# The second query group's output projection goes to the next attention unit, and the steps around it are numbered anew

## What is computed

```python
def reference(x, w_qkv, w_out, wg, w1, b1, w2, b2):
    xn = layernorm(x)
    ...
    qkv = einsum('bse,ehd->bshd', xn, w_qkv);  q, k, v = split(qkv, 3, axis=-1)
    logits = einsum('bqhd,bkhd->bhqk', q, k) / sqrt(64)
    probs = softmax(where(tril, logits, neg), axis=-1)
    attn = einsum('bshd,hde->bse', einsum('bhqk,bkhd->bqhd', probs, v), w_out)
    ...
    return x + attn + ffn
```

## Time and profile before

| | us |
|---|---|
| median of 3 runs | 3245.05 |
| lowest and highest | 3241.91, 3245.84 |
| the profiled execution | 3247.3 |
| span of its instructions | 3245.3 |
| PE busy | 3037.0 (94%) |
| DVE busy | 2254.5 (69%) |
| ACT busy | 1674.7 (52%) |
| POOL busy | 1612.6 (50%) |

### The profile page before, as it was taken

One profiled execution on the slowest core, in us unless ns is written; L12 is line 12 of the kernel. 1 busy time (PEld: TensorE's weight loads), 2 busy tenths in 40 slices (PEclk: granted clock), 3 DMA queues, 4 the chain that ended last, 5 costly groups with the idle time before them and its releaser, 6 DMA issues.

```text
span 3245.3 us, 64713 instructions
## 1 busy us (share of the span) xinstructions
PE 3037.0 (94%) x22677; PEld 2426.4 (75%) x22677; DVE 2254.5 (69%) x5152; ACT 1674.7 (52%) x3798; POOL 1612.6 (50%) x2384
## 2 busy tenths in 40 slices
PE   5589999999989999999999999999999999999996
PEld 3479998999977777777777777777777777777774
DVE  6844444444347778778877877787788778777875
ACT  2444444444445555555555555555555555555553
POOL 2132221222136665666566566656665665666563
PEclk7799999999999999999999999999999999999999
DMA  6022221222123323333233333333332333333232
GB/s 207 32 78 75 72 72 56 65 74 77 51 63 78 96 76 100 89 87 105 73 100 78 100 80 94 100 79 92 85 100 73 100 97 84 83 90 98 70 90 71
DMA packets 205201, 274.70 MB, mean 85 GB/s; under 512 B 61520, under 2 KB 161872, under 8 KB 204896
## 3 DMA queue, kind: packets, MB, share of 16 engines
q1 hardware_dynamic: 180288, 203.51, 22.6%
q0 software_dynamic: 24608, 67.17, 7.7%
HBM read 102.80 MB, written 33.55 MB: 42 GB/s over the span
## 4 chain that ended last, share of the span: by engine, by line
PE 55%; ACT 6%; DVE 5%; issue 4%; SPq 1%; DMA 0%; DVEq 0%
PE S L1272 14%; PE O L1309 13%; PE S L1188 8%; PE T L1285 8%; ACT pr L1347 4%; PE W L1223 3%; PE S L1203 3%; PE W L1203 3%; PE W L1188 3%; DVE pr L1404 2%; DVE kl L1435 1%; ACT kh L1362 1%; DVE ol L1449 1%; SPq L1125 1%; ACT oh L1372 1%
## 5 line engine op out<-in xcount | busy, mean ns | idle before, releaser
L1347 ACT ACTIVATE pr<-pr,negm 128x128 f32<-128x128 f32 (+7 forms) x1024 | 787.2, 770 | 756.5 <-DVE negm L1404 755.3
L1549 POOL TENSOR_SCALAR pr<-pr,rinv 128x128 f32<-128x128 f32 (+7 forms) x1024 | 759.6, 749 | 828.8 <-DVE rinv L1410 821.4
L1404 DVE CUSTOM_DVE_ANT_0 pr<-S,late 128x128 f32<-128x128 f32 (+7 forms) x1024 | 731.0, 751 | 48.1 <-PE S L1272 40.5
L1309 PE MATMUL O<-pT,vv 128*64 128x256 f32 (+1 forms) x5120 | 558.0, 364 | 14.0 <-DMA pT<-squares 13.2
L1309 PEld LDWEIGHTS O<-pT,vv 128*64 128x64 f32 x5120 | 345.7, 137 | 203.8 <-issue 24.1
L1339 DVE COPY pT<-T 128x512 f32<-128x512 f32 (+3 forms) x704 | 364.1, 540 | 147.3 <-PE O L1309 147.3
L1285 PE MATMUL T<-ident,pr 128*128 128x128 f32 x2688 | 420.6, 281 | 19.2 <-DVE pT L1339 18.6
L886 DVE TENSOR_TENSOR hl<-h,hh 128x512 fp32r<-128x512 f32 x256 | 191.5, 748 | 317.7 <-ACT hh L847 310.6
L1285 PEld LDWEIGHTS T<-ident,pr 128*128 128x128 f32 x2688 | 295.8, 140 | 133.5 <-issue 95.5
L843 ACT ACTIVATE h<-pH,b1c 128x512 f32<-128x512 f32 x256 | 175.9, 687 | 366.9 <-PE pH L773 353.0
L1272 PE MATMUL S<-kh,qh 64*128 64x512 f32 (+2 forms) x1536 | 319.6, 407 | 39.0 <-DVE negm L1404 34.9
(11 more groups left out here) (186 smaller groups left out, 6543.5 us busy)
## 6 DMA issues: line engine op xcount, KB each, us to landing
pT<-squares SPq DMA_DIRECT2D x768, 128.0 KB
pT<-squares POOLq DMA_DIRECT2D x256, 128.0 KB
y<-yb SPq DMA_DIRECT2D x128, 128.0 KB, 1.7
wr<-in_L_attn_w_qkv SPq DMA_DIRECT2D x128, 128.0 KB, 2.3
x<-in_L_attn_x SPq DMA_DIRECT2D x16, 512.0 KB, 5.4
xn<-xn SPq DMA_DIRECT2D x16, 512.0 KB, 5.1
w1r<-in_L_ffn_w SPq DMA_DIRECT2D x8, 1024.0 KB
w2r<-in_L_ffn_w SPq DMA_DIRECT2D x8, 1024.0 KB
```

The costliest lines, as they stand in the source:

```text
L1309: ins = e.matmul(O[hs, a:GQ], vv[n // 2 % 2][:, kt, vs], turned_p, start=(kt == 0), stop=(kt == KT - 1))
L1347: e.activation(pr[i][:, 0:w], pr[i][:, 0:w], ACT.Exp, bias=negm[:, i:i + 1], scale=-1.0, accum_out=rsum[:, i:i + 1]).then_inc(expd.sem, 1)
L1404: e.tensor_tensor_reduce(pr[i][:, 0:w], S[s % 2][:, off:off + w], late[:, SEQ - w:], 1.0, -MASKED, ALU.add, ALU.min, negm[:, i:i + 1]).the ...
L1549: e.tensor_scalar(pr[i][:, 0:width(s)], pr[i][:, 0:width(s)], rinv[:, i:i + 1], 1.0, ALU.mult, ALU.mult).then_inc(scaled.sem, 1)
```

## The change

The output projection o1 of group 1 leaves step 15 of its own unit and stands at step 2 of the next one (`NEXT = 1`: groups 1 to 3 are projected in the next unit, before it was 2 and 3). Its reader on DVE, the store of that quarter of the result and its refill follow. All the tables are new with it: o1's neighbours, `BANK_OF`, `AFTER` (group 0 at step 12 instead of 13, group 2 at step 6 of the next unit instead of 3), `SQUARE_LAG` 4 instead of 3, `POOL_AT`, and the chunks that ACT copies: eight instead of five, with 23 of a unit's 42 blocks instead of 10. No arithmetic is added or taken away.

```diff
-    KEPT_BY_ACT = {1, 10, 11, 13, 15}
+    KEPT_BY_ACT = {3, 7, 10, 11, 12, 13, 14, 15}
     KEPT_BY_DVE = set(range(CHUNKS)) - KEPT_BY_ACT
...
-    STEP_OF = {'p0': 0, 'v0': 1, 'xn': 1, 'v1': 4, 'p1': 6, 'p2': 6, 'p3': 6, 'o2': 9, 'o3': 12, 'o0': 14, 'o1': 15}
-    BANK_OF = {'p0': 0, 'p1': 1, 'p2': 0, 'p3': 2, 'o2': 2, 'xn': 0, 'v0': 2, 'o3': 2, 'v1': 0, 'o0': 2, 'o1': 2}
+    STEP_OF = {'p0': 0, 'v0': 0, 'o1': 2, 'p1': 3, 'p2': 3, 'p3': 4, 'v1': 4, 'xn': 7, 'o2': 8, 'o3': 12, 'o0': 14}
+    BANK_OF = {'p0': 0, 'p1': 0, 'p2': 1, 'p3': 2, 'o2': 2, 'xn': 2, 'v0': 2, 'o3': 2, 'v1': 1, 'o0': 2, 'o1': 2}
+
+    NEXT = 1
+    done_in = lambda n, g: n + (g >= NEXT)
...
-    POOL_AT = {'place0': 2, 'place1': 3, 'fetch0': 5, 'fetch1': 6, 'weigh': 9, 'add': 11, 'total': 15, 'split_w': 7, 'split_wv': 5}
+    POOL_AT = {'place0': 1, 'place1': 2, 'fetch0': 2, 'fetch1': 5, 'weigh': 8, 'add': 9, 'total': 13, 'split_w': 7, 'split_wv': 5}
...
-        SQUARE_LAG = 3
+        SQUARE_LAG = 4
...
-        AFTER = [13, 14, 19, 27]
+        AFTER = [12, 14, 22, 27]
...
                 if b > 0 and u == 0:
                     refill(b, 0)
-                    refill(b, 1)
...
                 if b > 0 and u == 0:
+                    store(b - 1, 1)
+                    refill(b, 1)
                     store(b - 1, 2)
...
                 if u == PAIRS - 1:
                     store(b, 0)
-                    store(b, 1)
...
-                of = n if g < 2 else n - 1
+                of = n if g < NEXT else n - 1
```

More of the change, by code:

```diff
@@ L947, in pieces @@
         there = {"p": n + 1 < UNITS, "x": n + AHEAD < TILES, "v": n + 1 < UNITS}
-        return [p for p in STEP_OF if there.get(p[0], n < UNITS if p in ("o0", "o1") else n > 0)]
+        return [p for p in STEP_OF if there.get(p[0], n < UNITS if p[0] == "o" and int(p[1]) < NEXT else n > 0)]
     class Pieces:
@@ L1127, in store @@
             def store(b, g):
-                e.wait_ge(dve.sem, dve.at(b * PAIRS + PAIRS - 1 + g // 2, f"o{g}"))
+                e.wait_ge(dve.sem, dve.at(done_in(b * PAIRS + PAIRS - 1, g), f"o{g}"))
                 e.dma_start(outv[:, b, 2 * g:2 * g + 2], res[:, 2 * g:2 * g + 2]).then_inc(stored[g].sem, 16)
@@ L1170, in _ @@
                     store(b, 0)
-                    store(b, 1)
             place(UNITS - 1)
-            for g in range(HT // 2, GROUPS):
+            for g in range(NEXT, GROUPS):
                 store(BATCH - 1, g)
@@ L1366, in group @@
                 e.wait_ge(pv.sem, pv.at(n, g + 1))
[L1368 to L1371, removed]
+                m, last = (n, g - 2) if g >= 2 else (n - 1, g + 2)
+                if m >= 0:
+                    e.wait_ge(filled.sem, filled.at(done_in(m, last), f"o{last}"))
                 e.activation(oh[g % 2][:], O[:], ACT.Copy).then_inc(ohi.sem, 1)
```

## The result

| | before | after |
|---|---|---|
| median, us | 3245.31 (3241.91 to 3245.84) | 3226.53 (3223.47 to 3228.04) |
| span of the profiled execution | 3245.3 | 3225.4 |
| ratio, 95% interval | | 0.9944 (0.9931 to 0.9956) |

The kernel is faster by 0.56%, 18.8 us of the forecast 44, with the right sign and less than half of the size. 3201 was the forecast and 3226.5 lies in the stated range, between the estimates for a late ACT (B, 3217) and a late DVE (C, 3233), but neither is what happened.

A forecast was written before the change was run, and what follows sets the result against it. PE was taken to bound the attention part, with its waits as the room. -0.66 - 0.20 + 0.20 = -0.66 us a unit, times 64 = -42.2, with the end -44, gave 3201 us from 3245.05; range 3172 to 3234.

The forecast's parts named there:

- B: Rival: ACT late at the unit's start, wait at chunk 12 0.45 us, net gain 0.41 a unit, 3217 us; chance 0.15.
- C: Rival: DVE late at step 8, 0.5 us more at step 10's scores, net gain 0.16 a unit, 3233 us; chance 0.08.
- PE bounds the attention part, and the waits decide, not DVE's load: Attention part: PE busy 34.3 of 35.7 us a unit; a new order can give back only its 1.4 us idle.
- rival E: DVE's copies, not the waits, decide: 13 blocks fewer, 2.2 us a unit, to about 3104 us; chance 0.02.
- The term of o1: Unit's end: PE's wait for group 1's remainder ol goes when o1 moves, -0.66 us a unit.
- The term of chunk 7: Step 9's transposes: with chunk 7's copy on ACT, row maxima start earlier and the wait for chunk 8 falls, -0.20 of 0.28 us.
- The wait at chunk 12: Transposes of step 10: PE newly waits for ACT's copy of chunk 10, +0.20 us a unit, bounds 0 and 0.5.
- The scores of step 10: PE's wait for step 9's row maximum stays at 0.43 us; term 0, bounds -0.1 and +0.5.
- Squares later: Squares one step later: placing DMAs still in time for group 3, distance about 12.7 us, some 2 us to spare; cost 0.
- Rival D: Placing DMAs become the bound at group 3: 3238 us, or slower at 3288; chances 0.03 no change or small gain, 0.09 slower.
- The changed neighbours: PE's starts where groups have new neighbours: may cost or give 0.1 us; cost 0.
- same work: Group 0's values stand ahead of chunk 7's transposes instead of behind them; counted at cost 0.

The follow-up runs named there:

- Experiment 2: The kernel before with only the new split of the chunk copies (ACT eight chunks, DVE eight): 3263.7 us, 1.0062.
- o1_early: `defer_xn` with o1 one step earlier, at step 1 behind xn instead of step 2: 3161.7 us, 0.9749 of the kernel before.
- Experiment 1: The kernel before with o1 alone moved to step 2 of the next unit, all other tables old: 3211.7 us, 0.9901.
- experiment 3: The changed kernel, two separate runs: squares back at three steps behind, 3219.1 us; or gathers back at steps 5 and 6, 3216.6 us.
- experiment 4: The changed kernel with the old split of the chunk copies (ACT 1, 10, 11, 13, 15) put back: 3283.0 us, 1.0125 of the changed kernel's predecessor.
- experiment 8: The changed kernel with squares at three steps, gathers late, and transposes of chunks 10 and 11 behind the next unit's first scores: 3175.7 us, 0.9794.
- g0_first: The kernel with o1 alone moved, plus group 0's values at step 12 instead of 13, ahead of chunk 7's transposes: 3238.3 us, 0.9986.
- experiment 5: The changed kernel with squares at three steps, old steps and banks of all pieces but o1, group 2's values at step 3: 3253.3 us, 1.0035.
- only_kept: The run of Experiment 2: the kernel before with only the new split of the chunk copies, 3263.7 us.
- fetch_late: The changed kernel with the gathers back at steps 5 and 6, their weighting at 9 and sum at 11: 3216.6 us, 0.9920.
- defer_xn: o1 alone moved, plus transposes of chunks 10 and 11 behind the next unit's first scores and xn in bank 1: 3170.0 us, 0.9772.

## Why the prediction was right and wrong, step by step

**PE bounds the attention part, and the waits decide, not DVE's load: right.** Experiment 2 took 13 blocks off DVE and the kernel got slower. The weight loads' busy share, on which rival E leaned, told nothing of the room: PEld is busy for 2426 us of the whole span before and 2432 in `o1_early`, while the unit went from 35.67 to 34.40 us by waits and distances alone.

**The term of o1: right in kind, too small.** -0.66 was read as idle time. The profile lets the transposes ahead last until their modelled end, but a projection can start 0.03 us after the last transpose. By the starts the wait was 0.91 us, a third more, so this error is on the good side and hid a part of the others. Experiment 1 shows the whole: -0.91, +0.25 at chunk 12, +0.16 of spacing, -0.49 us a unit.

**The term of chunk 7, -0.20: measured -0.08.** I let the row maxima start 0.2 us earlier. They start 1.80 us after the first score matmul instead of 1.90, with an idle time of DVE ahead that the scores end:

```profile
1498.32 1.23 DVE L1405 CUSTOM_DVE_ANT_0 pr<-S,late 128x1024 f32<-128x1024 f32 x1 [0.18 <-PE S L1274]
```

Only 0.1 us was there to win, since the scores themselves were the next thing late.

**The wait at chunk 12, +0.20: right** (+0.25; idle 0.19).

**The scores of step 10, 0: right** (+0.05).

**Squares later, 0: the step failed in its second half.** The distance between placing and use came out (12.7 forecast, 12.8 measured). But I took from the DMA share of one unit that the data had moved 10.8 us after the first issue, with 2 us to spare. By the semaphores the last landing was at 11.9 in that unit and at 11.4 in the mean, so there were 1.4. And I had gone through what stands ahead of the squares on DVE, and not through what the change puts beside them on POOL's queue. The gathers now run earlier among them, the last landing came at 12.6, and 0.10 us a unit was lost. With the gathers moved back the landing came at 11.9 and the loss was gone (experiment 3). Rival D was the right mechanism, at a sixth of the price that I gave it; experiment 4 shows it at 0.54 us.

**The changed neighbours, "may cost or give 0.1, cost 0": the step that failed most.** They cost 0.31 us a unit, 20 us. About half of it (0.16) comes with o1's own move, the rest with the new order of the pieces and of group 0 (0.14 to 0.15 between the ledgers of experiment 1 and of the changed kernel, about as much in experiment 8). PE uses its array in three shapes here: scores have 64 rows (64\*128 in the rows), values 64 columns (128\*64), all else is 128 by 128. Within one shape a run of transposes is followed after 0.03 us by a p or v piece or a projection; at a change of shape the next start comes 0.20 us after the last transpose or values matmul, and 0.32 after a p piece, where 0.23 is plain. The unit of before changes shape 20 times, that with o1 alone 21 times, that of after 23 times. `g0_first` adds such a change and lengthens its stretch by 0.15 us; group 0's move, which the prediction called "same work", is this change. `o1_early` takes one away and gains 0.11. The Trainium skill, TensorEngine Tiling (Array Packing), Key Properties, says that changing the tiling mode drains TensorE; the traces agree, with about 0.1 us a change, and 0.17 where it also breaks the start right behind a transpose. That the array is drained is the skill's word; what the runs show is the distance.

**The sum.** Forecast -0.66 = -0.66 - 0.20 + 0.20. Measured -0.28 = -0.91 - 0.08 + 0.25 + 0.05 + 0.10 + 0.31. The errors are +0.31 for the neighbours, +0.12 for chunk 7, +0.10 for the placing, +0.05 each for chunk 12 and step 10, and -0.25 for o1. That the range held the time is luck: it was drawn for rivals B and C, neither of which came, and the term that made most of the difference was not in it beyond 0.1 us.

**What the other tables are for.** Against o1 moved alone they lose 15 us. Yet they cannot be taken singly: without the new split the new order loses 56 us to late squares, copies and low parts (experiment 4), with the new split the old order loses 0.2 us at each of two places (experiment 2), and the split needs v0 ahead of chunk 14 (experiment 5). What stays open is how the 0.31 us divide over single neighbours beyond those named. The wait for the row maximum at step 10, 0.4 to 0.55 us in every kernel, was not attacked.

## To carry to other kernels

Cost a moved block by the distances from start to start of its old and its new neighbours, at both places, and count the changes between array shapes: a block between others of its own shape is cheaper than the same block elsewhere. Where a wait is taken away, its cover goes too: here the two T buffers that were behind it held PE for 0.6 us in experiment 1, while all the tables around it lost 15 us, and a large block between the transposes covered both. When DMAs have a due time, take their landing from many units and not from one, and look at all queues for what the change puts beside them, not only at when they are issued.

## What the runs showed of the hardware that I had not expected

- An idle time in front of a matmul can understate its wait: 0.66 us of idle stood for 0.91 us by the starts, and in `only_kept` 0.22 us at o0 had no row of PE at all.
- Sixteen placing DMAs of 128 KB landed 11.9 us after the first issue with two gathers issued at 5.9 and 9.9 us, and at 12.6 with these at 3.3 and 6.1 (means; `fetch_late` and the changed kernel).
- The same 22677 matmuls were 3022.5 us busy in `defer_xn`, 3037.0 in the kernel before and 3052.0 after the change, by their order and by waits that the modelled ends cover.
